# Another order in the fill of a six-layer linear-attention kernel with a routed expert gate

## The reference

```python
xn = layernorm(x)
s = xn
for i in range(6):
    n = layernorm(s) * ln1_w[i] + ln1_b[i]
    q, k, v = n @ wq[i], n @ wk[i], n @ wv[i]          # 8 heads of 16
    q = softmax(q, over the 16 of a head);  k = softmax(k, over the 1024 tokens)
    s = (q @ (k.T @ v)) @ wo[i] + bo[i] + s            # per head
    n = layernorm(s) * ln2_w[i] + ln2_b[i]
    h = n @ w1[i];  h = where(h >= 0, h, 0.01 * h)     # 512 wide
    s = h @ w2[i] + s
probs = softmax(xn @ router_w.T + router_b)            # 8 experts
e = argmax(probs)
y = (xn @ expert_w[e].T + expert_b[e]) * max(probs)
out = x + s * silu(y)
```

## Time and profile before

| | |
|---|---|
| median of 3 runs | 677.25 us (674.97 to 678.91) |
| profiled execution | 677.46 us, of which span 675.7 us |
| TensorE busy | 634.4 us (94%) |
| VectorE busy | 531.5 us (79%) |
| ScalarE busy | 402.5 us (60%) |
| GpSimd busy | 297.4 us (44%) |
| mean granted TensorE clock | 0.969 of full |

### The profile page before, as it was taken

How to read it: one execution, slowest core, us unless ns; L and a number is a source line. 1 busy time by engine, 2 the same in 40 slices (tenths; PEclk the granted TensorE clock), 3 DMA queues, 4 the chain that set the end, 5 groups by cost and what they waited for, 6 DMA issues and landing times.

```text
span 675.7 us, 12942 instructions
## 1 busy us (share of the span) xinstructions
PE 634.4 (94%) x4542; PEld 570.3 (84%) x4542; DVE 531.5 (79%) x1517; ACT 402.5 (60%) x700; POOL 297.4 (44%) x279
## 2 busy tenths in 40 slices
PE   5687669999999999999999999999999999999996
PEld 5476549889988988988988988988998988988985
DVE  5557857987897887897887897887897887988676
ACT  3553436756765755765765765765765765765563
POOL 4332486755343233243233243233243275786643
PEclk9768679999999999999999999999999999999999
DMA  8910010001000200210200210200210000000003
GB/s 287 349 50 1 10 39 17 29 24 60 2 1 1 63 1 2 63 43 22 63 0 0 62 42 20 63 2 1 63 48 16 16 25 17 25 24 17 24 2 124
DMA packets 29175, 29.03 MB, mean 43 GB/s; under 512 B 3265, under 2 KB 24769, under 8 KB 29122
## 3 DMA queue, kind: packets, MB, share of 16 engines
q1 hardware_dynamic: 26640, 24.12, 11.4%
q0 software_dynamic: 2048, 4.20, 2.1%
q10 hardware_dynamic: 434, 0.02, 0.0%
HBM read 17.85 MB, written 10.49 MB: 42 GB/s over the span
## 4 chain that ended last, share of the span: by engine, by line
PE 89%; DVE 4%; SPq 3%; issue 2%; POOL 1%; ACT 1%; DMA 1%; DVEq 0%; ACTq 0%
PE psY L428 25%; PE psT L341 12%; PE psH L346 7%; PE psH L347 7%; PE psH L348 6%; PE psT L469 6%; PE psM L525 6%; PE psS L500 6%; PE psM L474 6%; PE psY L362 1%; PE psS L399 1%; POOL sorted_x L1129 1%; PE psS L508 1%; PE psS L513 1%; PE psS L392 1%
## 5 line engine op out<-in xcount | busy, mean ns | idle before, releaser
L428 PEld LDWEIGHTS psY<-w_all,hid 128*128 128x128 f32 x1536 | 195.3, 191 | 19.2 <-issue 8.7
L428 PE MATMUL psY<-w_all,hid 128*128 128x128 f32 (+1 forms) x1536 | 203.5, 276 | 0.2 <-DVE X L899 0.2
L1112 POOL TENSOR_TENSOR rstd<-veps,minus_half 128x8 f32<-128x8 f32 x52 | 85.8, 1650 | 187.8 <-DVE veps L716 184.6
L927 DVE TENSOR_TENSOR hid<-psH,hsl 128x512 f32<-128x512 f32 x192 | 131.2, 684 | 41.4 <-ACT hsl L613 37.8
L613 ACT ACTIVATE hsl<-psH 128x512 f32<-128x512 f32 x192 | 114.1, 595 | 57.4 <-PE psH L348 54.9
L631 ACT ACTIVATE xh<-X,shift,rstd 128x128 f32<-128x128 f32 x280 | 116.9, 487 | 0.5 <-POOL shift L1115 0.5
L1166 POOL TENSOR_TENSOR xn_lo<-xn,xn_hi 128x512 fp32r<-128x512 f32 x46 | 57.8, 1278 | 103.5 <-DVE xn_hi L934 103.4
L346 PE MATMUL psH<-xn_hi,w_hi 128*128 128x512 f32 x184 | 86.6, 470 | 9.0 <-POOL xn_lo L1166 6.6
L699 DVE BATCH_NORM_STATS2 st<-X 128x6 f32<-128x128 f32 x384 | 80.5, 277 | 1.1 <-DMA w_all<-in_w_dram 1.0
L347 PE MATMUL psH<-xn_hi,w_lo 128*128 128x512 f32 x184 | 73.5, 399 | 0.0
L348 PE MATMUL psH<-xn_lo,w_hi 128*128 128x512 f32 x184 | 72.9, 396 | 0.0
(11 more groups left out here) (145 smaller groups left out, 1049.6 us busy)
## 6 DMA issues: line engine op xcount, KB each, us to landing
wb<-expert_rows SPq DMA_DIRECT2D x40, 128.0 KB, 2.1
w_all<-in_w_dram SPq DMA_DIRECT2D x12, 256.0 KB, 4.7
sorted_x<-zeros SPq DMA_DIRECT2D x5, 512.0 KB, 7.1
xs<-sorted_x SPq DMA_DIRECT2D x10, 256.0 KB, 3.0
sorted_y<-ys SPq DMA_DIRECT2D x10, 256.0 KB, 2.4
xraw<-in_x_dram SPq DMA_DIRECT2D x4, 512.0 KB, 6.5
out_dram<-xraw SPq DMA_DIRECT2D x3, 512.0 KB, 2.7
expert_rows<-expert_all SPq DMA_DIRECT2D x1, 1024.0 KB, 9.2
```

Of the source, the lines that this page charges most:

```text
L428: last = nc.tensor.matmul(tile(psY, t), tile(hid[:, i % NC, :], t), of_layer(w2_all, l, c * D, D), start=(c == 0 and t == 0), stop=(c == N ...
L927: nc.vector.tensor_tensor(hid[:, i % NC, :], psH[:, i % 2, :], hsl[:, i % 2, :], ALU.max) \
```

## The change

- SyncE loads the first layer's wk and wq right behind batch 0, and its wv and wo behind batch 1; each input batch has a semaphore of its own. VectorE waits for these four weights before slot 0 and for all others at the end of slot 0.
- VectorE normalises half of batch 0, ScalarE the other half; the statistics of batch 0's first norm come ahead of batch 1's input statistics, and ScalarE normalises batch 1 after the first tiles of xh.
- TensorE's transposes of the input and its logits products move to later places of slots 0 and 1, ScalarE's copies with them.
- `route` runs once, for all 32 tiles (256 columns), at place 7 of slot 1, in place of four times for 8 tiles. `top_weights` runs once, in slot 3, and its exponential at the end of slot 2.
- `ranks` moves to the end of slot 1. `places` is cut up: the results of `ranks` are copied out of PSUM near the start of slot 2, then four pieces follow hid 3, 4, 5 and 6 of slot 2, and the expert of every tile follows hid 3 of slot 3.
- GpSimd's scatters are 4 tiles at the end of slot 2, 8 in slot 3 and 10 each in slots 4 and 5.

The diff, cut to its core:

```diff
+            sp.dma_start(wk_all[:, 0, :], wk[0]).then_inc(sig("first_loaded"), 16)
+            sp.dma_start(wq_all[:, 0, :], wq[0]).then_inc(sig("first_loaded"), 16)
             for b in range(1, NBATCH):
                 sp.dma_start(xraw[:, b, :], x_in[b].rearrange("(p t) d -> p (t d)", p=P)) \
-                    .then_inc(sig("x_loaded"), 16)
+                    .then_inc(sig(f"x_loaded_{b}"), 16)
+                if b == 1:
+                    sp.dma_start(wv_all[:, 0, :], wv[0]).then_inc(sig("first_loaded"), 16)
+                    sp.dma_start(wo_all[:, 0, :], wo[0]).then_inc(sig("first_loaded"), 16)
...
             def route_step(n, i):                      # TensorE
-                if n == 0 and i in (1, 3, 6):
-                    normalised_tiles((1, 3, 6).index(i))
-                if n == 0 and i in (2, 4, 7):
-                    logits((2, 4, 7).index(i))
-                if n == 1 and i == 0:
+                if n == 0 and i == 3:
+                    normalised_tiles(0)
+                if n == 0 and i == 5:
+                    logits(0)
+                    normalised_tiles(1)
+                if n == 0 and i == 7:
+                    logits(1)
+                if n == 0 and i == 8:
+                    normalised_tiles(2)
+                if n == 1 and i == 2:
+                    logits(2)
+                if n == 1 and i == 3:
                     normalised_tiles(3)
-                if n == 1 and i == 1:
+                if n == 1 and i == 5:
                     logits(3)
-                if n == 1 and i == 6:
+                if n == 1 and i == 9:
                     ranks()
...
                 if isinstance(f, int) and f == 0 and i == 0:    # w2_step
-                    pe.wait_ge(sig("row_ready"), 1)
+                    pe.wait_ge(sig("place_step"), 2)
...
-            normalise_input(1)                         # ScalarE
             act.wait_ge(sig("ln1_shift"), 1)
             for k in range(4):
                 nc.scalar.activation(tile(xh1[:, 0, :], k), ...)
+            normalise_input(1)
...
+            def place_step(n, i):                      # VectorE, behind hid i
+                if n == 2 and i == 3:
+                    count_tokens()
+                if n == 2 and i == 4:
+                    pad_counts()
+                if n == 2 and i == 5:
+                    first_rows()
+                if n == 2 and i == 6:
+                    rows_of_tokens()
+                if n == 3 and i == 3:
+                    experts_of_tiles()
+                if n == 3 and i == 5:
+                    top_weights()
...
-            dve.wait_ge(sig("x_loaded"), 16 * (NBATCH - 1))
-            input_statistics(1, 0)
-            input_statistics(1, 1)
-            input_variances(1)
...
+            dve.wait_ge(sig("in_shift"), 1)
+            for t in range(NT // 2, NT):
+                last = nc.vector.tensor_scalar(xb(X, 0, t * P, P), xb(xraw, 0, t * P, P), rstd[:, 2, t:t + 1],
+                                               shift[:, 2, t:t + 1], ALU.mult, ALU.add)
+            last.then_inc(sig("first_half_ready"), 1)
+            dve.wait_ge(sig("first_half_ready"), 1)
+            norm1_half(0, 1)
             dve.wait_ge(sig("x0_ready"), 1)
             norm1_half(0, 0)
-            norm1_half(0, 1)
             token_statistics(0, "ln1", 2, 1)
+            dve.wait_ge(sig("x_loaded_1"), 16)
+            input_statistics(1, 0)
+            input_statistics(1, 1)
+            input_variances(1)
+            normalise_rest(0, 0, 0)
...
-                    elif attn:
-                        route_step(n, i)
+                        if isinstance(n, int):
+                            place_step(n, i)
+                    elif attn and n == 1 and i == 7:
+                        route()
...
                     nc.vector.tensor_tensor(xb(X, nbatch), xb(X, nbatch), psM[:, :], ALU.add) \
                         .then_inc(sig("x1_added"), 1)
+                if isinstance(n, int) and n == 2:
+                    take_ranks()
...
             dve.wait_ge(sig("param_loaded"), 16 * 2)
-            dve.wait_ge(sig("attn_loaded"), 16 * 4 * L)
-            dve.wait_ge(sig("ffn_loaded"), 16 * 2 * L)
+            dve.wait_ge(sig("first_loaded"), 16 * 4)
...
-                    if isinstance(n, int) and 1 <= n <= 4:      # GpSimd
-                        if n > 1:
-                            scatter(range(NT * (n - 1) + first, NT * (n - 1) + end))
-                        elif first == 6:
-                            scatter(range(0, NT))
+                    if isinstance(n, int) and n == 2 and first == 6:
+                        scatter(range(0, 4))
+                    if isinstance(n, int) and n == 3:
+                        scatter(range(4 + first, 4 + end))
+                    if isinstance(n, int) and 4 <= n <= 5:
+                        scatter(range(12 + 10 * (n - 4) + first, 12 + 10 * (n - 4) + (end if first < 6 else 10)))
```

More of the change, by code:

```diff
@@ L358, in logits @@
                 pe.wait_ge(sig("xn0T_ready"), b + 1)
-                wait(pe, "lg_ready", b)
                 for t in range(NT):
@@ L556, in normalise_input @@
                 act.wait_ge(sig("in_shift"), b + 1)
-                for t in range(NT):
+                for t in range(NT if b > 0 else NT // 2):
+                    if b == 0 and t == NT // 2 - 1:
+                        act.wait_ge(sig("first_half_ready"), 1)
                     last = nc.scalar.activation(xb(X, b, t * P, P), xb(xraw, b, t * P, P), ACT.Identity,
@@ L760, in places, with place_after, take_ranks @@
-            def places():
-                def after(step):
-                    dve.wait_ge(sig("place_step"), step)
-                def whole(a):
-                    return a[:, :, :].rearrange("p a b -> p (a b)")
-                last_of = running[:, :, TT - 1]
+            def place_after(step):
+                dve.wait_ge(sig("place_step"), step)
+            def take_ranks():
                 dve.wait_ge(sig("ranks_done"), 1)
-                dve.wait_ge(sig("ones_ready"), 1)
                 nc.vector.tensor_copy(in_tile[:, :, :],
@@ L773, in places, with count_tokens, whole @@
                     .then_inc(sig("place_step"), 1)
-                after(1)
+                nc.vector.tensor_copy(place[:, :, :], psY[:, 0:TT * E].rearrange("p (t e) -> p t e", e=E)) \
+                    .then_inc(sig("place_step"), 1)
+            def count_tokens():
+                def whole(a):
+                    return a[:, :, :].rearrange("p a b -> p (a b)")
+                place_after(2)
                 nc.vector.tensor_tensor_scan(whole(running), ones256[:, :], whole(in_tile), 0.0, ALU.mult, ALU.add) \
                     .then_inc(sig("place_step"), 1)
-                after(2)
+                nc.vector.tensor_tensor(lg[:, :, :], lg[:, :, :],
+                                        lmax[:, :].unsqueeze(2).broadcast_to([P, TT, E]), ALU.subtract) \
+                    .then_inc(sig("lsub_ready"), 1)
+                place_after(3)
                 nc.vector.tensor_copy(count[:, 0:1], running[:, 0, TT - 1:TT])
@@ L1068, in slot @@
                     gated(NBATCH - 1, 0)
+                if isinstance(n, int) and n == 0:
+                    dve.wait_ge(sig("attn_loaded"), 16 * 4 * (L - 1))
+                    dve.wait_ge(sig("ffn_loaded"), 16 * 2 * L)
                 if attn and j == (0 if isinstance(n, int) and n < 4 else 1):
```

135 lines of the change are left out of this document (64 added, 71 removed).

## The result

The changed kernel takes 660.67 us (median of 4 runs, 658.80 to 660.86) against 678.08 (674.97 to 679.52) for the kernel before in the same session: a ratio of 0.974 (95% interval 0.970 to 0.978). The profiled execution took 658.80 us, 656.9 of them span, against 675.7 of span before.

The account below looks back on a forecast made before the run. TensorE bounds from the first feed-forward product, a chain through all engines before it. Terms -0.1 -9.1 -11.8 +2.0 -1.0 +2.7 +1.1 +0.4 = -15.8 us, taking 677.46 to 661.7, predicted as 661.5; range 655.5 to 668.5.

Parts of the forecast that it names:

- The bound: From the first feed-forward product (91.84 us) TensorE bounds the run; before it, a chain through all engines does.
- The start, -0.1: Until first xnT: VectorE's wait for all weights goes, but its own order still delays wv_s; -0.1 us, ends -1 to +0.5.
- Slot 0, -9.1 at full clock: First xnT to end of xh transposes: chain no longer stands behind the router, 23.5 us against 32.64.
- Slot 1, -11.8: To the first feed-forward product: later logits, no 6.60 us wait behind scatters, tables gone; 21.8 us against 33.55.
- The clock, +2.0, ends 0 and +8: Slots 0 and 1: sums assume 2.4 GHz; a mean granted clock of 0.93 adds 2 us, 0.77 adds 8.
- Slot 2, +2.8: Tables delay gT (+2.7 us), scatters delay xn_lo (+1.1), higher clock at the slot's start gives back 1.0.
- rival C: Slots 2 and 3: VectorE's queue bounds, 18 table operations each held 0.5 us by GpSimd; +9, 667.5 us; chance 0.05.
- Slot 3, +0.4: Three table operations (1.2 us) against 0.85 us of slack before gT; +0.4 us.
- A: The tables cost nothing and the clock holds: -22, 655 us; chance 0.14.
- B: Clock stays as low as before: +8 in place of +2, and slot 2 begins low (+1); 668 us; chance 0.18.
- D: Slots 2 to 5: scatters slow beside busy VectorE, 2.3 us each, make it slower than before; +21, 682 us; chance 0.02.
- E: Slots move as a whole by VectorE's start; only the scatters' 6.60 us go; 671 us; chance 0.05.

Follow-up runs that it names:

- a_filled: Kernel after, with five more VectorE reductions, results unused, between hid 3 and gT of slot 2: 661.90 us, ratio 0.977.
- a_stage_early: Kernel after, with wk_s, wv_s and two parameter copies made ahead of the statistics of batches 2 and 3: 655.25 us, ratio 0.967.
- a_weights_late: Kernel after, with all weights loaded in the old order and waited for at the old place: 660.81 us, ratio 0.975.
- a_keep_late: Kernel after, with GpSimd's two copies of X to gate placed behind the last input deviations: 660.41 us, one execution.
- a_router_old: Kernel after, with the router's transposes, logits products and ScalarE copies at their old places, routing still one pass: 665.49 us, ratio 0.982.
- b_scatter: Kernel before, with only the changed schedule of the scatters (4 at the end of slot 2, 8, 10, 10): 670.29 us, ratio 0.988.
- best: Kernel after, with the edits of a_stage_early, a_tables_moved and a_keep_late together: 657.13 us, ratio 0.970.
- best_warm: best, with 26 more identity transposes on TensorE before the first xh transposes and 26 behind them: 653.13 us, ratio 0.965.
- after_again: Kernel after, unchanged, measured once more as a yardstick: 660.07 us (6 runs), ratio 0.974.
- a_warm: Kernel after, with 26 more identity transposes on TensorE ahead of the first xh transposes and 44 behind: 658.60 us, ratio 0.972.
- a_tables_moved: Kernel after, with tables moved later, row_index at the start of slot 3, and 11, 11, 10 scatters in slots 3 to 5: 658.32 us, ratio 0.972.

## Why the prediction was right, step by step

**The bound.** That TensorE limits all from the first feed-forward product on, so that each microsecond there is gained or lost for good, held: all later slots took 534.6 us as before, and in a_filled a stand of 1.64 us more at gT made the slot 1.64 us longer.

**The start, -0.1, measured -0.6.** The mechanism was right (wv_s, in VectorE's own list; a_stage_early takes it away and xnT comes 4.56 us sooner). The load of the weights itself is worth 0.3 us of it (a_weights_late); the rest I put down to the new order of the statistics, which no run undoes. The term for the two GpSimd copies, 0.8 us, was too large: they cost 0.38 (a_keep_late).

**Slot 0, -9.1 at full clock, measured -7.6.** The chain was timed well: mix product at 19.65 us after xnT. From there to the end only two groups ran at the lower clock, 3.40 in place of 2.05 most of all, and 25.07 stands for 23.5. Two things in the working do not hold. It says that its sums are at 2.4 GHz, but the 7.1 us to expk were taken from the kernel before, where the k product took 3.43 us; at full clock it takes 1.98 (slot 1). And it gives the places of the transposes and logits a part in the gain that they do not have: by a_router_old they net about nothing in this slot.

**Slot 1, -11.8, measured -12.2.** Right, and both parts show: b_scatter alone gives 8 us over the whole kernel; in a_router_old the old places cost 7.6 us in this slot between its xnT's, part of it by the clock.

**The clock, +2.0, ends 0 and +8.** Against the 23.5 of the working, slot 0 paid 1.6 us in one profiled execution (25.07) and 3.8 in the other (27.29); slot 1 paid nothing in either. That the term fits is in part luck, for what the clock costs is more than that. best and best_warm differ only in transposes of no use ahead of slot 0; from xnT to the end of the transposes of xh, best takes 25.06 us at a clock of 0.80, as the kernel after does, best_warm 21.31 at 1.00. A slot 0 at the full clock throughout is thus nearer to 21.3 us than to 23.5. And slot 1, from one xnT to the next, is 20.52 us at 1.00 in the kernel after, but 23.16 at 0.85 in a_keep_late, which has the same code there; a_weights_late, a_stage_early and best_warm show 23.2 as well, after_again, a_filled, a_warm and best 20.5. In order, the first slot of best and of best_warm and slot 1 of a_keep_late:

```profile
20.34:45.40 25.06, 22.69 (x142) 19.39 (x142) 17.41 (x58) 14.89 (x29) 11.79 (x12) 0.80 0.63 220
20.34:41.65 21.31, 18.54 (x144) 16.31 (x142) 17.41 (x56) 14.89 (x29) 11.80 (x12) 1.00 0.75 260
49.69:72.85 23.16, 19.46 (x131) 17.50 (x131) 15.62 (x49) 13.04 (x21) 7.96 (x7) 0.85 0.00 1
```

**Slot 2, +2.8, measured +1.5: the one step mis-sized.** The clock at its start gave back 0.98 (25.23 to 24.25 busy; forecast 1.0) and the stand behind the scatters was 1.05 (forecast 1.1). The stand at gT was 1.39 and not 2.7. I had counted 11 operations at the mean of 0.315 us from before, 3.5 us. They took 2.3 us (81.22 to 82.54 and 85.07 to 86.09). Of the difference 0.6 us is the scan, 0.68 us where before it had taken 1.28; the rest is that the ten beside it are the short ones of the 21. The reason for the scan's 1.28 was in the trace of before, and the prediction denied it ("no row of before shows that pair together"). It does; kernel before, slot 1:

```profile
72.61 1.93 POOL L1195 TENSOR_TENSOR qsm<-qe,qrec 128x1024 f32<-128x1024 f32 x1
...
73.81 1.28 DVE L775 TENSOR_TENSOR_SCAN running<-ones,in_tile 128x256 f32<-128x256 f32 x1
```

The scan, with two operands in SBUF, began beside qsm and ended 0.55 us after it. My mean had that wait in it, and I added the risk of another on top (rival C). In the new place the scan runs at 81.22 with GpSimd idle, as most of the tables do; a_filled shows that the stand follows VectorE's time one to one, so the smaller sum explains the smaller stand.
The Trainium skill (SBUF — State Buffer, "SBUF: two separate sides") says that such a VectorE instruction and a GpSimd one hold the shared ports in turn, each for its whole length. The rows agree, here and at first_row in a_tables_moved (1.25 us for 0.15 beside xn_lo).

**Slot 3, +0.4, measured +0.3.** TensorE waits 0.18 us there for gT, and in all but that the slot is full.

**The rivals.** A, that the tables cost nothing, is out by the two waits. B, a clock as low as before, is out in the kernel after, 0.80 and 1.00 in the two stretches; with the router's products at their old places (a_router_old) slot 1 has 0.76. C is out: of the tables in slot 2 only one, at 88.30 beside qsm, was held, 0.64 us for the 0.42 that it took before with GpSimd idle, and it stands behind gT. D needed scatters of more than 2.15 us; they start 1.27 to 1.52 us apart beside a busy VectorE (91.66, 93.18, 94.45, 95.79), and later slots did not change. E, only the 6.60 us, would have been 671; b_scatter, which takes only these away, has 670.29, and the change is 10 us better.

That the sum is -18.8 in the profiled execution and -17.4 between the medians, for -15.8 forecast, is the gT stand (1.3), the start (0.5), slot 1 (0.4), the clock (0.4) and small ones; the profiled execution was the fastest of its four.

## What to carry to other kernels

Take indirect DMAs off an in-order queue wherever the bound engine waits for something behind them: that one reordering gave 8 of the 17 us. Before moving small work into a stretch that another engine bounds, find the slack of the instruction behind it (here 0.85 us for gT): beyond it the work is paid one to one (1.64 us for 1.64). Moving it to the head of the next slot took 2.8 us from one slot and put 1.8 on the other. And look at the granted clock before a difference of 2 or 3 us is put down to an edit: one fall of it is as large. Do not take a mean duration from a stretch in which some of the group were held by another engine: look at each operation and at what GpSimd did beside it.

## What the runs showed of the hardware that I had not expected

- VectorE operations on two SBUF operands beside a GpSimd one: scan 1.28 us for 0.68, negmean 0.53 for 0.17, first_row 1.25 for 0.15, `running` plus `pad_before` 0.64 for 0.42. A four-tile normalisation of one SBUF operand with scalars was held as well, beside GpSimd's copies: 2.56 us, where the same line takes 1.11 elsewhere.

```profile
41.79 2.02 POOL L1169 COPY gate<-X 128x1024 f32<-128x1024 f32 x2
...
41.83 2.56 DVE L883 TENSOR_SCALAR xh<-X,rstd,shift 128x128 f32<-128x128 f32 x4
```

- The granted clock differs between executions of one kernel, with the same instructions in the same order: 0.77 or 0.70 in 20:45, worth 2.2 us, and in slot 1 either 1.00 or 0.85, worth 2.6. Transposes of no use on an idle TensorE ahead of slot 0 gave 1.5 to 2 us in one kernel, with executions that overlap, and a clear 4 in another; eight more in each of two holes of slot 1 gave nothing that can be measured.
- In the combination of three edits ScalarE waited 2.56 and 3.08 us for something that the trace does not name, though each edit alone, and all other kernels here without the three together, show no such wait. It was not settled.
